# Two expert routings: the eight largest logits of a tile and their positions from VectorE, the router's bias by TensorE, the gather index ahead of the experts' table

## The chip, the cores and the metric

The kernel runs on one core of one Trainium2 chip. The metric is the device time of one execution in microseconds, as the median of several runs; lower is better. One execution was also taken by the profiler, and all the rows below come from it.

## The reference, cut to what matters

The input `x` holds T = 2048 tokens of width D = 256 (two sequences of 1024). Four blocks are added to it in turn:

```python
x = x + xattn0(layernorm(x), ctx)     # 16 heads of 64, 77 keys per sequence, RMS-normalised q and k
x = x + moe0(layernorm(x))            # 8 experts, hidden width 256, 2 experts per token
x = x + linear1(layernorm(x), ctx)    # x @ W1.T + mean(ctx) @ W2.T + b
x = x + moe1(layernorm(x))            # 8 experts, hidden width 1024, 2 experts per token
```

Each mixture of experts routes in the same way; only the second has a router bias:

```python
logits = x @ router_w (+ router_b)
probs = softmax(logits)
top_p, top_e = top_k(probs, 2)
y = sum over the token's two experts of top_p * (gelu(x @ w1[e] + b1[e]) @ w2[e] + b2[e])
```

## The kernel before, in words

Tokens stand in NT = 16 tiles of 128, one token per partition. A product of two numbers is made from fp16 halves, high and low, as three TensorE products (`three`), and weights are scaled by WS = 64. Each engine has one hand-written order of work, in software-pipelined loops over steps `s`; a function called with `s - 5` handles the tile that entered five steps earlier. Semaphores tie the engines together.

The stages in order of time are these. First the attention's keys and values are prepared. Then a loop over the 16 tiles (`for s in range(NT + 9)`, on every engine) does the query projection (`q_proj`), scores (`scores`, `shift`), exponentials, their sums (`sums`, L1124 to L1131, on VectorE), the normalisation of the weights by GpSimd (`norm_weights`, L648), transposes of the weights on TensorE with their split into halves by ScalarE (`pt_hi`, L857) and VectorE (`pt_lo`, L1136), the product with the values (`attn`), its addition to the residual (`add_attn`, L1146), the second layer norm's statistics (`stats`), and for an older tile the router's logits: TensorE's `logits(0, ln1, i)` at step i + 8 writes eight numbers per token into a small place of bank 5, and VectorE's `logits(0, i)` (L1153), in the same step, scales them into `lg`. `sums` ends with a reciprocal (L1130) and a multiplication by PS = 1024 (L1131). VectorE's `split_lo` (L1095) makes the low halves of expert weights in the odd steps, GpSimd's (L616) in the even ones.

Then comes `route(0)`. VectorE finds the largest logit, its place, the second largest and its place over all 16 tiles at once (L1235 to L1248, twelve linked operations), which ends in `hot`, a table of ones; then the two gates (L1255 to L1259). TensorE counts the tokens of each expert (RANKS). VectorE turns counts into places (L1267 to L1293), TensorE turns places into token numbers (`tokens_done`), VectorE makes the table of experts per slot (L1299 to L1304) and last the gather index (L1307). TensorE goes on with idle products (`idle_work`) meanwhile. GpSimd waits for the one semaphore `routed` and gathers rows by that index.

The first experts follow: 39 slots of 128 rows each. Four weight chunks are split first (L1095), then per slot VectorE copies the expert's weights (`first_weights`, L1370), TensorE transposes the gathered rows and multiplies, ScalarE does the gelu. SyncE's queue writes each slot's result (`keep_y`, L509) and loads the last big weight chunks (`stage`). Its loop over slots issues `stage(NCH - 1)` at the second-to-last slot step, ahead of the last five `keep_y`.

Then a loop over 16 tiles gathers the two results of each token (L712), adds them with their gates (L1444, L1450), applies the linear block (`add_linear`, L1432), layer norm, and the second router: TensorE's `logits(1, ln3, i)` at step i + 7, read by VectorE's `logits(1, i)` (L1157) at step i + 9, which adds the bias `rbb`. Then `route(1)` by the same code, and the second experts, 39 slots again, with `slot_weights` (L1333) on VectorE and scatter-adds into the output by GpSimd (L725).

VectorE's part of the attention loop, as far as order matters here:

```python
if LEAD <= s - 4 < NT:      # L1197
    pt_lo(s - 4, 0)
    pt_lo(s - 4, 1)
...
if 0 <= s - 6 < NT and (PRE + s - 6) % 2:      # L1207
    split_lo(PRE + s - 6)
```

Of the kernel before, what the change touches and what calls it, by code (L numbers as in the profile page):

```python
# [7 lines left out]
ALU = mybir.AluOpType  # L8
# [3 lines left out]
P = 128  # L12
# [51 lines left out]
def build(nc, x, ctx_t, wq, wk, wv, scale_q, scale_k, wo, bo, rw0, w_in0, b_in0, w_out0, b_out0,  # L64
# [29 lines left out]
    with ExitStack() as ctx:  # L94
# [104 lines left out]

        back = lg[:, :, :].rearrange("p t e -> p (t e)")[:, 0:NQS[1]].bitcast(U32)  # L200
# [132 lines left out]
        LOG = [bank[5][:, 400:400 + E]] * 2  # L333
        LOG1 = [bank[4][:, 400:400 + E], bank[5][:, 400:400 + E]]
# [83 lines left out]
        def _(sp):  # L418
# [96 lines left out]
            for j in range(NSLOTS[0] + 4):  # L515
# [35 lines left out]
        def _(pool):  # L551
# [41 lines left out]
            g.memset(pb2[:, NS:NS + 1], PS)  # L593
            g.memset(pb01[:, :, NS:NS + 1], PS)
# [9 lines left out]
            link(g.iota(first8[:, :], pattern=[[-1, E]], base=E, channel_multiplier=0,  # L604
# [82 lines left out]
            def slot_rows(layer):  # L687
                pool.wait_ge(sem("routed"), layer + 1)
# [52 lines left out]
        def _(act):  # L741
# [110 lines left out]
            def pt_hi(i, n):  # L852
                a, b = groups[n]
                act.wait_ge(sem("weights_tr"), NG * i + n + 1)
                if i >= 2:
                    act.wait_ge(sem("attn_done"), i - 1)
                s_.activation(pt[:, i % 2, 0, a:b, :], bank[6 + (NG * i + n) % 2][:, 0:(b - a) * P].rearrange(  # L857
                    "p (c t) -> p c t", t=P), ACT.Copy).then_inc(sem("pt_hi"), 1)
# [35 lines left out]
            def route(layer):  # L894
                act.wait_ge(sem("route_shift"), 2 * layer + 1)
                r = routes[layer]
                s_.activation(r[:, 7 * P:7 * P + NT * E], r[:, 0:NT * E], ACT.Exp).then_inc(sem("route_exp"), 1)
                act.wait_ge(sem("route_shift"), 2 * layer + 2)
                s_.activation(r[:, 1104:1104 + NT], r[:, 1152:1152 + NT], ACT.Exp).then_inc(sem("route_exp"), 1)
# [26 lines left out]
            act.wait_ge(sem("routed"), 1)  # L926
# [49 lines left out]
        def _(dve):  # L976
# [147 lines left out]
            def sums(i):  # L1124
# [5 lines left out]
                link(v.reciprocal(rs[:, i % 2, :], rs[:, i % 2, :]))  # L1130
                v.tensor_scalar(rs[:, i % 2, :], rs[:, i % 2, :], PS, None, ALU.mult).then_inc(sem("row_sums"), 1)  # L1131

            def pt_lo(i, n):
                a, b = groups[n]
                dve.wait_ge(sem("pt_hi"), NG * i + n + 1)
                v.tensor_tensor(pt[:, i % 2, 1, a:b, :], bank[6 + (NG * i + n) % 2][:, 0:(b - a) * P].rearrange(  # L1136
                    "p (c t) -> p c t", t=P), pt[:, i % 2, 0, a:b, :], ALU.subtract).then_inc(sem("pt_lo"), 1)
# [12 lines left out]
            def logits(layer, i):  # L1150
                dve.wait_ge(sem("logits_done"), NT * layer + i + 1)
                if layer == 0:
                    v.tensor_scalar(lg[:, i, :], LOG[i % 2], 1.0 / WS, None, ALU.mult).then_inc(sem("logits_read"), 1)  # L1153
                else:
                    if i == 0:
                        dve.wait_ge(sem("rb_loaded"), 16)
                    v.scalar_tensor_tensor(out=lg[:, i, :], in0=LOG1[i % 2], scalar=1.0 / WS, in1=rbb[:, :],  # L1157
                                           op0=ALU.mult, op1=ALU.add).then_inc(sem("logits_read"), 1)

            for s in range(NT + 9):  # L1160
# [21 lines left out]
                if 0 <= s - 8 < NT:  # L1182
                    logits(0, s - 8)
# [21 lines left out]
                if s == 3:  # L1205
                    split_lo(3)
                if 0 <= s - 6 < NT and (PRE + s - 6) % 2:  # L1207
                    split_lo(PRE + s - 6)

            def route(layer):  # L1210
# [10 lines left out]
                ex, m1, m2, best = cut(0), r[:, 1024:1024 + NT], r[:, 1152:1152 + NT], r[:, 1088:1088 + NT]  # L1221
                oh = [cut(1), cut(2)]
                cand, masked = cut(3), cut(4)
# [5 lines left out]
                cur = lg[:, :, :]  # L1229
                f8 = first8[:, None, :].to_broadcast([P, NT, E])  # L1230

                def all_experts(m):
# [638 lines left out]
```

## Time and profile before

| what | us |
|---|---|
| median of 3 runs | 650.48 |
| lowest, highest run | 647.2, 650.99 |
| the profiled execution, whole | 651.32 |
| its span, first to last instruction | 649.5 |
| mean granted TensorE clock in it, share of full speed | 0.931 |

The span is what the rows below divide up; around it lie 1.8 us of start and end. A row of a timeline gives start, duration, engine, line, operation, output <- input, shapes and count, and in brackets the idle time of that engine just before it and what released it. Unlinked instructions of one engine overlap in it by some hundredths of a microsecond.

### The profile page before, as it was taken

What the parts mean: (1) busy time and instruction counts of PE and PEld (TensorE: products, weight loads), DVE (VectorE), ACT (ScalarE), POOL (GpSimd) and SP (SyncE); (2) the same over time, 40 slices, a digit from 0 to 9 for tenths busy, and PEclk for the clock granted to TensorE, in tenths of its full rate; (3) what the DMA queues carried; (4) which work ended last, traced back from release to release, by engine and by line L of the source; (5) the groups of instructions that cost most, each with busy time, mean ns of one, the idle gap of its engine ahead of it and who ended that gap; (6) DMA issues with size and microseconds to landing.
All of it is one profiled execution on the core that took longest, in us unless ns stands there. A gap on an engine that the chain in (4) does not pass through costs nothing.

```text
span 649.5 us, 17761 instructions
## 1 busy us (share of the span) xinstructions
PE 537.8 (83%) x6478; PEld 482.4 (74%) x6478; DVE 522.7 (80%) x1052; ACT 369.4 (57%) x597; POOL 370.9 (57%) x300
## 2 busy tenths in 40 slices
PE   5899999999998754798981655299999999999991
PEld 4898898989898642677760444179999999999991
DVE  4877899999988859699986998777788777777861
ACT  3735476766755442799975788344444444444441
POOL 8157598898888622775505883044555565554332
PEclk9989999999988885899996799689999999999997
DMA  8600223333231344798772642544545544444422
GB/s 300 166 11 17 75 59 82 91 82 92 74 99 49 98 101 168 220 302 274 221 236 90 180 120 67 155 94 57 80 78 76 75 79 80 78 77 75 62 25 25
DMA packets 74228, 71.30 MB, mean 110 GB/s; under 512 B 44257, under 2 KB 64482, under 8 KB 73890
## 3 DMA queue, kind: packets, MB, share of 16 engines
q1 hardware_dynamic: 63250, 50.59, 27.7%
q0 software_dynamic: 10896, 19.58, 16.1%
q8 instruction: 56, 0.92, 0.6%
q14 instruction: 26, 0.21, 0.1%
HBM read 44.83 MB, written 16.53 MB: 94 GB/s over the span
## 4 chain that ended last, share of the span: by engine, by line
PE 45%; DVE 23%; issue 9%; ACT 8%; POOL 8%; DMA 4%; DVEq 1%; POOLq 0%; ACTq 0%; SPq 0%
PE banks L1491 43%; POOL heads L636 2%; DVE w_region L1141 2%; POOL w_region L643 2%; POOL w_region L648 2%; DMA out<-slot_region,lg 2%; DVE slot_region L1136 2%; DVE wb_region L1014 2%; DVE w_region L1128 1%; ACT wb_region L836 1%; PE banks L1710 1%; DVE heads L1111 1%; DVE w_region L1118 1%; ACT slot_region L906 1%; ACT wb_region L781 1%
## 5 line engine op out<-in xcount | busy, mean ns | idle before, releaser
L1491 PE MATMUL banks<-w_region,wb_region 128*128 (+1 forms) x1000 | 118.7, 276 | 10.0 <-DMA wb_region<-wk 7.5
L725 POOL DMA_INDIRECT out<-slot_region,lg x39 | 67.0, 1718 | 98.4 <-ACT slot_region L959 72.9
L1491 PE MATMUL banks<-w_region 128*128 128x128 f16 (+5 forms) x1484 | 111.3, 233 | 13.5 <-DVE w_region L1141 8.1
L1491 PEld LDWEIGHTS banks<-w_region 128*128 128x128 f16 (+3 forms) x1484 | 106.3, 127 | 18.7 <-DVE w_region L1141 11.7
L1491 PEld LDWEIGHTS banks<-w_region,wb_region 128*128 128x128 f16 (+1 forms) x1000 | 99.7, 105 | 20.5 <-issue 10.7
L1491 PE MATMUL banks<-slot_region,staging 128*128 128x128 f16 x1872 | 110.9, 219 | 0.9 <-ACT slot_region L906 0.7
L1491 PEld LDWEIGHTS banks<-slot_region,staging 128*128 128x128 f16 x1872 | 107.5, 98 | 2.2 <-ACT slot_region L906 0.9
L912 ACT ACTIVATE wb_region<-wb_region 128x1024 f32<-128x1024 f32 x39 | 41.3, 1058 | 90.2 <-DVE wb_region L1342 90.2
L1333 DVE COPY staging<-w_region 128x2048 f16 x78 | 57.3, 737 | 40.6 <-PE banks L1491 39.8
L681 POOL DMA_INDIRECT slot_region<-normed_rows,index x39 | 45.5, 1166 | 36.2 <-DVE index L1307 16.6
L1491 PE MATMUL banks<-w_region,slot_region 128*128 128x256 f16 x480 | 58.6, 283 | 1.9 <-DVE slot_region L1136 1.9
L681 POOL DMA_INDIRECT slot_region<-gated_rows,index x39 | 41.6, 1068 | 26.1 <-DVE index L1307 14.5
L1491 PEld LDWEIGHTS banks<-w_region,slot_region 128*128 128x128 f16 x480 | 48.2, 102 | 9.0 <-DVE slot_region L1136 2.0
L712 POOL DMA_INDIRECT wb_region<-sorted_y,slots x32 | 32.9, 1030 | 31.7 <-DMA sorted_y<-slot_region 23.6
L1491 PE MATMUL banks<-wb_region,w_region 128*128 (+1 forms) x302 | 49.0, 301 | 1.3 <-DVE w_region L1080 0.8
L636 POOL TENSOR_TENSOR heads<-heads,neghalf 128x16 f32<-128x16 f32 x16 | 47.7, 2983 | 2.5 <-DVE heads L1104 2.5
L1342 DVE SCALAR_TENSOR_TENSOR wb_region<-banks,b_s 128x1024 f32<-128x1024 f32 x39 | 47.2, 1209 | 1.1 <-PE banks L1491 1.1
L1349 DVE TENSOR_TENSOR wb_region<-wb_region 128x1024 f16<-128x1024 f32 x39 | 47.2, 1211 | 0.6 <-ACT wb_region L921 0.6
L648 POOL TENSOR_TENSOR w_region<-w_region 128x1232 f32<-128x1232 f32 x16 | 36.2, 2261 | 16.0 <-DVE w_region L1131 15.4
L857 ACT ACTIVATE slot_region<-banks 128x512 f16<-128x512 f32 (+1 forms) x48 | 23.5, 522 | 35.0 <-PE banks L1614 35.0
L921 ACT ACTIVATE wb_region<-wb_region 128x1024 f16<-128x1024 f32 x39 | 40.6, 1042 | 0.1
L643 POOL TENSOR_TENSOR w_region<-w_region,heads 128x1232 f32<-128x1232 f32 x16 | 38.5, 2406 | 1.3
(236 smaller groups left out, 1033.9 us busy)
## 6 DMA issues: line engine op xcount, KB each, us to landing
staging<-w_t SPq DMA_DIRECT2D x22, 512.0 KB, 4.3
sorted_y<-slot_region SPq DMA_DIRECT2D x39, 128.0 KB, 4.0
w_region<-w_t SPq DMA_DIRECT2D x8, 512.0 KB, 5.7
x_res<-x SPq DMA_DIRECT2D x4, 512.0 KB, 7.8
staging<-w_in SPq DMA_DIRECT2D x4, 512.0 KB, 3.7
normed_rows<-w_region SPq DMA_DIRECT2D x16, 128.0 KB, 1.9
staging<-w_out SPq DMA_DIRECT2D x4, 512.0 KB, 4.0
gated_rows<-wb_region SPq DMA_DIRECT2D x16, 128.0 KB, 2.2
```

The source lines that it names most:

```text
L636: link(g.tensor_tensor(v, v, neghalf[:, 0:1].to_broadcast([P, NH]), ALU.pow))
L643: g.tensor_tensor(p_rows(i), p_rows(i), rq[:, i % 2, :, None].to_broadcast([P, NH, L]), ALU.mult).then_inc(sem("scores_scaled"), 1)
L648: g.tensor_tensor(p_rows(i), p_rows(i), rs[:, i % 2, :, None].to_broadcast([P, NH, L]), ALU.mult).then_inc(sem("weights_ready"), 1)
L681: g.indirect_dma_start(out=m.rows[:, j % m.RING, a, :].bitcast((F16, U32)[layer]), out_offset=None, in_=rows_dram[layer], in_offset=bass.I ...
L712: g.indirect_dma_start(out=ring[:, i % n, c, :], out_offset=None, in_=y_dram, in_offset=bass.IndirectOffsetOnAxis(ap=slots[:, i, c:c + 1], ...
L725: g.indirect_dma_start(out=out, out_offset=bass.IndirectOffsetOnAxis(ap=back[:, j:j + 1], axis=0), in_=m.y[:, j % m.YB, 0, :], in_offset=N ...
L912: s_.activation(v, v, ACT.Gelu_apprx_tanh).then_inc(sem("gelu"), 1)
L921: s_.activation(m.hh[:, j % 2], v, ACT.Copy).then_inc(sem("h_hi"), 1)
L1333: v.tensor_copy(w_slot[:, :, half], src[:, :, half]).then_inc(sem("slot_weights"), 1)
L1342: v.scalar_tensor_tensor(out=m.g[:, j % 2], in0=hidden(m, j), scalar=1.0 / WS, in1=bias[:, :, None].to_broadcast([P, m.HC, m.SW]), op0=ALU ...
L1349: v.tensor_tensor(m.hl[:, j % 2], m.g[:, j % 2], m.hh[:, j % 2], ALU.subtract).then_inc(sem("h_lo"), 1)
L1491: return t.matmul(o, a, b, start=start, stop=stop)
```

## The change

The two routings no longer search all tiles at once. For each tile VectorE runs `max` (the eight largest values, sorted; of eight logits all of them) and `max_index` (their positions), straight from the PSUM banks where TensorE left the logits. The logits of the first ten tiles stay in one bank side by side, those of the last six in other banks, and VectorE's calls (`tops`) stand at the ends of the steps given by `tops_at`, from step 18 on. The reads of `lg` step by step are gone. The two tables of ones come from comparing positions with 0 to 7. The second router's bias enters as two products with an identity matrix, of its halves. In the first routing the gates are computed behind the index and the experts' table, in the second ahead of the counts. The gather index stands ahead of the experts' table, and `routed` counts twice per routing: GpSimd waits for the index, TensorE and ScalarE for both. The factor PS moves out of `sums` into `pt_hi` (as a scale) and `pt_lo` (a fused multiply and subtract), and the constant column of the weights is 1 instead of PS. `stage(NCH - 1)` moves behind the loop over slots.

```diff
+        SHARED = 10
+        def log_home(layer, i):
+            if i < SHARED:
+                return bank[(5, 2)[layer]][:, 384 + E * i:384 + E * (i + 1)]
+            return bank[((1, 2, 3, 4, 1, 2), (3, 3, 4, 5, 2, 3))[layer][i - SHARED]][:, 400 + E * (i % 2):400 + E * (i % 2 + 1)]
+        def bank_full(layer, i):
+            return SHARED if i < SHARED else max(i + 1, SHARED + 2 * layer)
+        def tops_at(layer, s):
+            if layer == 0:
+                return {NT + 2: range(0, 5), NT + 3: range(5, 10), NT + 4: range(10, 12), NT + 5: range(14, 15)}.get(s, ())
+            return {NT + 2: range(0, 3), NT + 3: range(3, 6), NT + 4: range(6, 10), NT + 5: range(10, 12),
+                    NT + 6: range(12, 14), NT + 7: range(14, 15), NT + 8: range(15, 16)}.get(s, ())
...
                 elif j == NSLOTS[0] - 1:
-                    stage(NCH - 1)
                     stage(NCH - LATE + 1)
                 if j >= 4:
                     keep_y(j - 4)
+            stage(NCH - 1)
...
-                link(v.reciprocal(rs[:, i % 2, :], rs[:, i % 2, :]))
-                v.tensor_scalar(rs[:, i % 2, :], rs[:, i % 2, :], PS, None, ALU.mult).then_inc(sem("row_sums"), 1)
+                v.reciprocal(rs[:, i % 2, :], rs[:, i % 2, :]).then_inc(sem("row_sums"), 1)
...
+            def tops(layer, tiles):
+                for i in tiles:
+                    dve.wait_ge(sem("logits_done"), NT * layer + bank_full(layer, i))
+                    sorted_at = mark(v.max(out=lg[:, i, :], in_=log_home(layer, i)))
+                if tiles:
+                    dve.wait_ge(sem("dve_chain"), sorted_at)
+                for i in tiles:
+                    v.max_index(out=ranked_of(layer)[:, i, :], in_max=lg[:, i, :], in_values=log_home(layer, i)).then_inc(
+                        sem("logits_read"), 1)
...
-                if 0 <= s - 8 < NT:
-                    logits(0, s - 8)
+                if s == NT + 5:
+                    tops(0, range(12, 14))
+                if s == NT + 7:
+                    tops(0, range(15, 16))
...
+                tops(0, tops_at(0, s))
                 if 0 <= s - 6 < NT and (PRE + s - 6) % 2:
                     split_lo(PRE + s - 6)
...
-                link(v.tensor_reduce(m1, cur, axis=AX.X, op=ALU.max))
...
-                v.tensor_tensor(hot.rearrange("p t e -> p (t e)"), oh[0], oh[1], ALU.add).then_inc(sem("hot"), 1)
+                for c in range(2):
+                    chosen = v.tensor_tensor(te(both[:, c, :]), ranks[:, c, :, None].to_broadcast([P, NT, E]),
+                                             first8[:, None, :].to_broadcast([P, NT, E]), ALU.is_equal)
+                    if c:
+                        link(chosen)
+                v.tensor_tensor(hot.rearrange("p t e -> p (t e)"), both[:, 0, :], both[:, 1, :], ALU.add).then_inc(
+                    sem("hot"), 1)
+                v.tensor_tensor(te(ex), lg[:, :, :], lg[:, :, 0:1].to_broadcast([P, NT, E]), ALU.subtract).then_inc(
+                    sem("route_shift"), 1)
...
+                if layer == 1:
+                    gates_of()
                 dve.wait_ge(sem("counts_done"), layer + 1)
...
+                dve.wait_ge(sem("tokens_done"), layer + 1)
+                found, later = bank[6][:, 0:NQ], bank[6][:, NQ:2 * NQ]
+                v.tensor_scalar(index[:, 0:NQ], found, -1.0, 0.0, ALU.add, ALU.max).then_inc(sem("routed"), 1)
                 if layer == 0:
                     link(v.tensor_scalar(slots[:, :, :], where, ALMOST_HALF, None, ALU.add))
...
-                link(v.tensor_scalar(expert[:, 1, 0:NSLOT], es, float(2 * DC * moes[layer].H), None, ALU.mult))
-                dve.wait_ge(sem("tokens_done"), layer + 1)
+                v.tensor_scalar(expert[:, 1, 0:NSLOT], es, float(2 * DC * moes[layer].H), None, ALU.mult).then_inc(
+                    sem("routed"), 1)
+                dve.wait_ge(sem("routed"), 2 * (layer + 1))
+                if layer == 0:
+                    gates_of()
...
-                if 0 <= s - 9 < NT:
-                    logits(1, s - 9)
+                tops(1, tops_at(1, s))
...
-                if i >= 7:
-                    pe.wait_ge(sem("logits_read"), i - 6)
...
+                for n in range(2 * layer):
+                    mm(home, ident_h[:, :], rb_halves[:, n, :], n == 0, False)
```

## Rows read from the trace of the kernel before

**Rows 1.** Stages: busy us of each engine, granted clock, DMA share, GB/s.
```profile
78.00:188.00 110.00, 105.44 (x1340) 99.66 (x1337) 103.64 (x194) 75.70 (x116) 96.80 (x57) 1.00 0.29 79
...
260.00:341.00 81.00, 69.46 (x860) 56.20 (x858) 72.51 (x173) 68.23 (x135) 41.94 (x38) 0.98 0.82 251
...
411.00:428.00 17.00, 7.28 (x63) 4.40 (x63) 13.16 (x39) 1.82 (x4) 3.07 (x4) 0.54 0.47 135
428.00:618.00 190.00, 189.48 (x2601) 179.63 (x2602) 150.33 (x216) 91.62 (x109) 96.84 (x70) 1.00 0.49 76
```

**Rows 2.** The chain of waits by engine, whole span.
```profile
PE 45%; DVE 23%; issue 9%; ACT 8%; POOL 8%; DMA 4%; DVEq 1%; POOLq 0%; ACTq 0%; SPq 0%
```

**Rows 3.** The chain of waits, two steps of the attention loop: start, us, what.
```profile
104.66 0.18 DVE w_region L1131
...
104.92 2.25 POOL w_region L648
...
116.71 0.07 DVE lg L1153
```

**Rows 4.** VectorE's timeline, a step of the attention loop.
```profile
206.75 0.15 DVE L1153 TENSOR_SCALAR lg<-banks 128x8 f32<-128x8 f32 x1
206.83 1.11 DVE L1111 TENSOR_REDUCE heads<-banks 128x12 f32<-128x924 f32 x1
```

**Rows 5.** VectorE's timeline, first routing.
```profile
242.76 0.17 DVE L1153 TENSOR_SCALAR lg<-banks 128x8 f32<-128x8 f32 x1 [0.44 <-PE banks L1491]
242.96 0.29 DVE L1235 TENSOR_REDUCE w_region<-lg 128x16 f32<-128x128 f32 x1
...
246.52 0.29 DVE L1248 TENSOR_TENSOR w_region<-w_region 128x128 f16<-128x128 f32 x1
246.74 0.28 DVE L1255 TENSOR_REDUCE w_region<-w_region 128x16 f32<-128x128 f32 x1
...
248.12 0.17 DVE L1267 TENSOR_SCALAR w_region<-banks 128x8 f32<-128x8 f32 x1 [0.61 <-PE banks L1491]
...
255.65 0.20 DVE L1307 TENSOR_SCALAR index<-banks 128x39 uint32<-128x39 f32 x1
```

**Rows 6.** VectorE's timeline, the end of the attention loop (steps 18 to 20).
```profile
221.66 1.27 DVE L1136 TENSOR_TENSOR slot_region<-banks,slot_region 128x512 f16<-128x512 f32 x2
224.22 0.43 DVE L1146 SCALAR_TENSOR_TENSOR x_res<-banks,x_res 128x256 f32<-128x256 f32 x1 [1.28 <-PE banks L1491]
...
229.31 1.22 DVE L1095 SCALAR_TENSOR_TENSOR w_region<-staging,w_region 128x1024 f16<-128x1024 f32 x1
```

**Rows 7.** TensorE's timeline at the last tile's attention product, and that stretch's clock.
```profile
232.12 5.11 PE L1491 MATMUL banks<-w_region,slot_region 128*128 128x256 f16 x30 [1.94 <-DVE slot_region L1136]
...
232.00:234.00 2.00, 1.88 (x9) 1.30 (x10) 0.29 (x3) 1.51 (x3) 1.90 (x3) 0.54 0.58 221
```

**Rows 8.** TensorE's timeline, the last token products, and the third slot's transposes.
```profile
254.19 0.71 PE L1491 MATMUL banks<-w_region 128*128 128x39 f16 x16 [0.35 <-DVE w_region L1293]
...
265.38 0.40 PE L1710 MATMUL banks<-ident_h,slot_region 128*128 128x128 f16 x4 [2.41 <-DMA slot_region<-normed_rows,index]
```

**Rows 9.** The chain of waits at the first experts' end, and DMA issues with landing.
```profile
340.71 3.28 DMA sorted_y<-slot_region
...
normed_rows<-w_region SPq DMA_DIRECT2D x16, 128.0 KB, 1.9
```

**Rows 10.** VectorE's timeline, the second router's loop and routing.
```profile
395.89 0.69 DVE L1014 TENSOR_TENSOR wb_region<-wb_region 128x256 f16<-128x256 f32 x1 [0.18 <-ACT wb_region L781]
...
403.26 0.41 DVE L1432 SCALAR_TENSOR_TENSOR x_res<-banks,x_res 128x256 f32<-128x256 f32 x1
...
405.60 0.42 DVE L1432 SCALAR_TENSOR_TENSOR x_res<-banks,x_res 128x256 f32<-128x256 f32 x1
...
410.87 0.17 DVE L1157 SCALAR_TENSOR_TENSOR lg<-banks,rbb 128x8 f32<-128x8 f32 x1 [0.71 <-PE banks L1491]
...
414.63 0.29 DVE L1248 TENSOR_TENSOR slot_region<-slot_region 128x128 f16<-128x128 f32 x1
```

More of the change, by code:

```diff
@@ L857, in pt_hi @@
                 s_.activation(pt[:, i % 2, 0, a:b, :], bank[6 + (NG * i + n) % 2][:, 0:(b - a) * P].rearrange(
-                    "p (c t) -> p c t", t=P), ACT.Copy).then_inc(sem("pt_hi"), 1)
+                    "p (c t) -> p c t", t=P), ACT.Copy, scale=PS).then_inc(sem("pt_hi"), 1)
             for s in range(NT + 9):
@@ L1135, in pt_lo @@
                 dve.wait_ge(sem("pt_hi"), NG * i + n + 1)
-                v.tensor_tensor(pt[:, i % 2, 1, a:b, :], bank[6 + (NG * i + n) % 2][:, 0:(b - a) * P].rearrange(
-                    "p (c t) -> p c t", t=P), pt[:, i % 2, 0, a:b, :], ALU.subtract).then_inc(sem("pt_lo"), 1)
+                v.scalar_tensor_tensor(out=pt[:, i % 2, 1, a:b, :], in0=bank[6 + (NG * i + n) % 2][
+                    :, 0:(b - a) * P].rearrange("p (c t) -> p c t", t=P), scalar=PS, in1=pt[:, i % 2, 0, a:b, :],
+                    op0=ALU.mult, op1=ALU.subtract).then_inc(sem("pt_lo"), 1)
             def q_lo(i):
@@ L1148, in add_attn, with ranked_of @@
                 dve.wait_ge(sem("attn_added"), i + 1)
[L1150 to L1158, printed above, removed]
+            def ranked_of(layer):
+                return routes[layer][:, 3 * P:3 * P + NT * E].bitcast(U32).rearrange("p (t e) -> p t e", e=E)
+            def tops(layer, tiles):
[7 more added lines that the diff above has]
+                        sem("logits_read"), 1)
             for s in range(NT + 9):
@@ L1303, in route @@
                 link(v.tensor_copy(expert[:, 0, 0:NSLOT], es))
-                link(v.tensor_scalar(expert[:, 1, 0:NSLOT], es, float(2 * DC * moes[layer].H), None, ALU.mult))
-                dve.wait_ge(sem("tokens_done"), layer + 1)
-                found, later = bank[6][:, 0:NQ], bank[6][:, NQ:2 * NQ]
-                v.tensor_scalar(index[:, 0:NQ], found, -1.0, 0.0, ALU.add, ALU.max).then_inc(sem("routed"), 1)
+                v.tensor_scalar(expert[:, 1, 0:NSLOT], es, float(2 * DC * moes[layer].H), None, ALU.mult).then_inc(
+                    sem("routed"), 1)
+                dve.wait_ge(sem("routed"), 2 * (layer + 1))
+                if layer == 0:
+                    gates_of()
                 if layer == 1:
@@ L1438, in _ @@
                 split_lo(k)
+            dve.wait_ge(sem("rb_loaded"), 16)
+            link(v.tensor_scalar(rb_halves[:, 0, :], rbb[:, :], WS, None, ALU.mult))
+            link(v.scalar_tensor_tensor(out=rb_halves[:, 1, :], in0=rbb[:, :], scalar=WS, in1=rb_halves[:, 0, :],
+                                        op0=ALU.mult, op1=ALU.subtract))
             for s in range(NT + 9):
```

82 lines of the change are left out of this document (34 added, 48 removed).

## The prediction

> **What bounds the kernel now.** I read the stages first, then the chain of waits, then each engine's timeline where the change touches it. From 428 to 618 us TensorE is busy 189.5 of 190 us at a granted clock of 1.00, its 2.4 GHz level, so the second experts are a fixed block that only starts earlier or later [rows 1]. The chain agrees: TensorE 45%, VectorE 23% of the span [rows 2]. In the attention loop (78 to 188) no engine alone is the bound: TensorE is busy 105.4, VectorE 103.6, GpSimd 96.8 of 110 us [rows 1], and the chain passes from VectorE's sums to GpSimd's normalisation and back [rows 3]. In a routing (411 to 428) TensorE is busy 7.3 of 17 us and VectorE 13.2: a serial chain of small VectorE operations with TensorE waiting, so what is cut there moves everything behind it [rows 1]. The first experts (260 to 341) have VectorE 72.5, TensorE 69.5 of 81 us, DMA 0.82 [rows 1]; nothing in their steady part changes.
>
> The sum is made against the profiled execution's 651.32 us (span 649.5 and 1.8 around it), which lies 0.84 above the median 650.48.
>
> **Attention loop: two operations less on the chain.** The chain shows the multiplication by PS 0.18 long with its link directly ahead of GpSimd's normalisation [rows 3]; without it GpSimd starts about 0.20 earlier. This sits on the chain once in two steps, five times between 78 and 188. The read of the logits appears on it with 0.07, four times [rows 3]. Together 5 x 0.20 + 4 x 0.07 = 1.3 us gained. In the other step of each pair GpSimd is itself still busy when the sums come, so nothing more is gained there. The scale in `pt_hi` and the fused `pt_lo` keep their shapes; I cost them at nothing. Bounds: 0 (another wait takes over) to 2.6.
>
> **The price of one tile's search.** No row of before shows `max` or `max_index`. The second takes in eight values and then searches the bank, so I count a tile as three small steps. Unlinked 128x8 steps start 0.08 apart (206.75, then 206.83), though each lasts 0.15 [rows 4]; linked small steps stand 0.20 apart (242.76, then 242.96) [rows 5]. So a tile costs between 0.16 (two steps of 0.08) and 0.60. I take 0.27, three steps of 0.09, nearest to rows 4 because within `tops` nothing is linked but the one wait between the two loops, which I put at 0.1 per group.
>
> The Trainium skill, "VectorE: DVE Perf Modes", § The DRAIN you can't avoid and § Rules for kernel authors, says that the next VectorE operation starts only when the last one's pipe is empty, and to keep the count of operations small: with full lengths of 0.155 a tile would cost 0.47. Rows 4, with 0.08 between starts, speak against that for short steps; what it would make of the time is the second rival's nearer half.
>
> **First routing, the end of the attention loop.** Ten of the 16 searches stand where VectorE is waited for.
> - Step 18: five tiles, 5 x 0.27 + 0.1 = 1.45, between `pt_lo` (221.66 to 222.93) and `add_attn` at 224.22, ahead of which VectorE idles 1.28 [rows 6]. With one logits read (0.08) gone, 0.1 is left over.
> - Step 19: 1.45 ahead of `split_lo` at 229.31 [rows 6]. What follows, `add_attn` and `pt_lo` of the last tile, is what TensorE waits for with 1.94 idle before 232.12 [rows 7]; so 1.45 - 0.08 = 1.4 late.
> - TensorE's product at 232.12 takes 5.11 with a granted clock of 0.54 in its first 2 us, mostly the 1.2 GHz level [rows 7]. Idle longer before it, it may run more of it there: at 1.2 GHz throughout, 30 x 256 columns are 6.4 us, an estimate from the shape in that row. I take 0.3 of the possible 1.3.
> - Tiles 10 to 14 fall into waits of VectorE, but tile 14 stands ahead of `split_lo` (1.22) and must wait for logits that come after it now; so that the last tile's search starts 0.55 late. Itself it takes 0.25 more than the 0.20 of the read it replaces (three dependent steps).
> - The twelve linked operations from 242.96 to the end of `hot` at 246.81 are 3.85 us [rows 5]. Left are two comparisons and one addition, 0.22 + 0.33 + 0.29 = 0.84: 3.0 gained.
> - The gates (from 246.74 to the start of the 0.61 of idle, 0.8 us [rows 5]) were hidden behind TensorE's counts; behind the index they delay only VectorE's weight splits.
> - The index: token products end at 254.90 [rows 8], the index ran at 255.65 [rows 5]. In front of the table it is 0.65 earlier.
>
> Sum to the index: 0.1 + 1.4 + 0.3 + 0.55 + 0.25 - 3.0 - 0.65 = -1.05. The gathers follow; the third slot waits 2.41 on its gather [rows 8]. VectorE itself, with table and gates behind the index, comes free earlier only by some 1 us less than the gathers, and it has to copy weights for the first slot; I take 0.35 off: -0.7.
>
> **End of the first experts.** `stage(NCH - 1)`, 512 KB, shared the DMA engines with the last results: the last `keep_y` takes 3.28 on the chain [rows 9]. An equal transfer of 128 KB, the `normed_rows` writes, takes 1.9 [rows 9]. Behind the loop on SyncE's queue the load no longer runs ahead of five `keep_y`. 1.0 gained of at most 1.4; its cover is the wait for the first gathered results, and if ScalarE's split came later than that, 1 us would be lost instead.
>
> **Second routing.** In the loop before it VectorE waits 0.18 for ScalarE in each step [rows 10], so dropping the logits reads gains nothing. At its end, three tiles at 0.91 (with the wait) stand ahead of `add_linear` at 403.26 and three ahead of that at 405.60 [rows 10], each less 0.08: about 1.5 late, since the layer norm of the last tile follows from them. Bias products: 0.1 on the last tile. The last search: 0.25 more. From 411.07, 0.20 behind the last read, to the end of `hot` at 414.92 [rows 10] 3.85 become 0.84: -3.0. The gates now end 0.2 behind the counts, because the exponential starts later; the index gains 0.25, because the table already hid most of that wait. Sum: 1.5 + 0.1 + 0.25 - 3.0 + 0.2 - 0.25 = -1.2.
>
> **Sum.** -1.3 - 0.7 - 1.0 - 1.2 = -4.2: 647.1 against 651.32; against the median 650.48, 646.3.
>
> **The rivals.**
> 1. *The searches hide better and are cheaper.* At 0.18 a tile (two short steps), step 18 hides wholly, step 19 costs 0.9, the second loop's groups 1.0 instead of 1.5, and the last tiles 0.1 less each: 1.3 less in all. With the loop's gain at its bound, 2.6, it is 2.6 more than forecast: 643.7. For it: rows 4. Against: a search of eight numbers for eight values is hardly one short step.
> 2. *The searches are slow and become the end of both loops.* At 0.60 a tile a group of five is 3.1: step 18 costs 1.7, step 19 3.0, the clock 0.8, the last tile 1.2, against 3.65 gained: +3.0 where I have -0.7. In the second loop groups of three are 1.9, so 3.7 late, and the nine tiles behind them (5.4) outlast the last logits by 2: with the same other terms about +3.2 where I have -1.2. Total 646.3 + 3.7 + 4.4 = 654.4, slower than before. It decides from about 0.45 a tile on, where the total is zero. At the skill's 0.47 the time would be the same as before. For it: linked steps at 0.20 [rows 5], and the order of work that puts ten tiles ahead of awaited operations [rows 6]. Against: nothing links them.
> 3. *The shorter first routing does not reach the slots.* The slots follow VectorE's splits, or the gathers land no earlier because the loads move with them; and the last `keep_y` keeps its 3.28. Then the two gains 3.65 and 1.0 are spent on less: +0.7 + 1.0, 648.0; with a loop gain of 0 also, 649.3. For it: VectorE's 72.5 of 81 us in that stage [rows 1]. Against: the wait of 2.41 on a gather [rows 8].
>
> **How the numbers follow.** Forecast 0.50, rival 1 0.25, rival 2 0.10, rival 3 0.15. The range reaches from 641.5 (rival 1 and the keep of 1.4, and clock dips of 1 to 2 us that fall differently) to 651.0, which leaves out most of rival 2 and some of the deepest gains. A measurement of this kernel, whose three runs lie within 0.6%, tells about 1% from no change. Faster by over 1% means under 644.0: half of rival 1 and some of the forecast, 0.24. Slower by over 1% means over 657.0: only the far part of rival 2, 0.05. The rest is 0.71.
>
> **What would show it.** Right: between a tile's searches starts about 0.09 apart; `hot` 0.84 behind the last search; the index directly behind `tokens_done`; the attention product of the last tile about 1.5 later against its loop, in a loop 0.27 shorter per two steps; the last `keep_y` near 2.3. Wrong: starts 0.2 apart, a `split_lo` of the last steps several us late, the first slots waiting on VectorE's copies instead of gathers, or an attention loop with an unchanged period.

## The result, and the profile after

The changed kernel takes 640.48 us (median of four runs, 640.08 to 642.68) against 650.59 for the kernel before in the same comparison: the recorded ratio is 0.9868, 95% interval 0.9834 to 0.9903 (the two medians alone, of four runs each, divide to 0.984). The forecast was 646.3 with a range from 641.5. So the direction was right and the gain, 10.1 instead of 4.2, more than twice as large; the median lies 1 us under the lower end of the range. The profiled execution took 640.1, its span is 638.4, the mean granted clock 0.933.

The stages of the changed kernel (columns as in [rows 1]; the attention loop 1 us earlier than there, the first experts 7 and in 80 us instead of 81, the second routing and the second experts 11), and its chain by engine:

```profile
77.00:187.00 110.00, 105.73 (x1343) 99.90 (x1340) 102.40 (x177) 76.29 (x117) 97.84 (x57) 1.00 0.29 80
253.00:333.00 80.00, 68.58 (x862) 54.95 (x859) 75.14 (x175) 68.65 (x135) 41.31 (x37) 1.00 0.81 251
400.00:417.00 17.00, 8.93 (x84) 5.48 (x84) 12.62 (x45) 2.94 (x5) 4.29 (x6) 0.53 0.52 149
417.00:607.00 190.00, 189.57 (x2602) 179.73 (x2603) 150.55 (x215) 91.55 (x108) 95.01 (x70) 1.00 0.47 76
```

```profile
PE 45%; DVE 21%; POOL 10%; issue 9%; ACT 9%; DMA 4%; DVEq 1%; POOLq 0%; ACTq 0%; SPq 0%
```

The second experts are the same block of 189.6 busy us, only earlier, and VectorE's share of the chain falls from 23% [rows 2] to 21%. VectorE's timeline shows the searches and the short routing, to be laid beside [rows 5, 6]:

```profile
218.25 0.45 DVE L1178 MAX8 lg<-banks 128x8 f32<-128x8 f32 x5
218.73 0.09 DVE L1182 MATCH_VALUE_LOAD w_region<-lg,banks 128x8 f32 x1
218.81 0.17 DVE L1182 FIND_INDEX8 w_region<-lg,banks 128x8 uint32<-128x8 f32 x1
218.89 0.07 DVE L1182 MATCH_VALUE_LOAD w_region<-lg,banks 128x8 f32 x1
...
219.79 0.42 DVE L1167 SCALAR_TENSOR_TENSOR x_res<-banks,x_res 128x256 f32<-128x256 f32 x1 [0.26 <-PE banks L1518]
...
224.89 0.46 DVE L1178 MAX8 lg<-banks 128x8 f32<-128x8 f32 x5
...
226.10 1.21 DVE L1116 SCALAR_TENSOR_TENSOR w_region<-staging,w_region 128x1024 f16<-128x1024 f32 x1
...
238.59 1.21 DVE L1116 SCALAR_TENSOR_TENSOR w_region<-staging,w_region 128x1024 f16<-128x1024 f32 x1
239.71 0.17 DVE L1178 MAX8 lg<-banks 128x8 f32<-128x8 f32 x1
...
240.72 0.29 DVE L1263 TENSOR_TENSOR w_region<-w_region 128x128 f16<-128x128 f32 x1
...
249.14 0.20 DVE L1318 TENSOR_SCALAR index<-banks 128x39 uint32<-128x39 f32 x1 [0.81 <-PE banks L1518]
```

A group of five runs from 224.89 to 226.10, 1.21 in all: five maxima in 0.46, then a pair for each position, 0.14 from start to start. The first group leaves VectorE 0.26 of its 1.28 idle ahead of tile 13's addition; the second stands wholly ahead of the split at 226.10. Tile 14's split (238.59) does delay the last maximum, as feared. `hot` ends 1.3 behind the start of the last maximum, and the index comes directly behind the token products.

The chain in the attention loop has one small operation less ahead of GpSimd, as against [rows 3]:

```profile
103.64 0.27 DVE w_region L1151
103.90 0.07 issue
103.97 2.25 POOL w_region L670
```

TensorE's timeline at the first slots, against [rows 8]: the first slot waits for VectorE's copy of its weights, and the third slot's transposes have no wait at all.

```profile
254.14 0.40 PE L1740 MATMUL banks<-ident_h,slot_region 128*128 128x128 f16 x4 [0.22 <-DMA slot_region<-normed_rows,index]
256.78 0.84 PE L1518 MATMUL banks<-slot_region,w_region 128*128 128x128 f16 x12 [2.25 <-DVE w_region L1394]
257.59 0.38 PE L1740 MATMUL banks<-ident_h,slot_region 128*128 128x128 f16 x4
```

VectorE's timeline at the second loop's end, against [rows 10]: two groups of three ahead of awaited additions, and the gates waiting 0.37 for the exponential.

```profile
393.28 0.31 DVE L1178 MAX8 lg<-banks 128x8 f32<-128x8 f32 x3
...
394.07 0.41 DVE L1456 SCALAR_TENSOR_TENSOR x_res<-banks,x_res 128x256 f32<-128x256 f32 x1
...
403.20 0.29 DVE L1263 TENSOR_TENSOR slot_region<-slot_region 128x128 f16<-128x128 f32 x1
...
404.07 0.29 DVE L1275 TENSOR_REDUCE slot_region<-slot_region 128x16 f32<-128x128 f32 x1 [0.37 <-ACT slot_region L919]
```

**A shift that no edit made.** Two traces can be compared landmark by landmark. Between the two first ones TensorE's clock differs where nothing was changed. The stretch of the attention loop in the kernel before, in its first profile (columns as in [rows 1]):

```profile
190.00:192.00 2.00, 2.00 (x24) 2.00 (x24) 2.00 (x4) 1.11 (x1) 0.82 (x2) 0.80 0.62 176
192.00:194.00 2.00, 2.00 (x21) 1.94 (x22) 1.22 (x4) 0.60 (x2) 0.81 (x1) 0.50 0.24 94
194.00:196.00 2.00, 2.00 (x22) 2.00 (x20) 1.97 (x6) 1.97 (x3) 1.54 (x2) 0.50 0.00 0
```

and the same stretch in its second profile (`e0`, below):

```profile
192.00:194.00 2.00, 2.00 (x37) 1.99 (x37) 1.93 (x7) 1.16 (x2) 0.43 (x1) 1.00 0.41 156
194.00:196.00 2.00, 2.00 (x35) 1.96 (x33) 1.97 (x3) 1.94 (x4) 2.00 (x2) 1.00 0.00 0
```

TensorE is busy throughout these rows in both, yet in the first it gets 0.50, its 1.2 GHz level, from 192 to 198 us, and does 21 products in 2 us instead of 37. TensorE's idle time just before, 0.93 of the 2 us from 188, is the same in the second profile (0.94). The reductions over the heads just behind it on VectorE come 1.9 later, counted as in the table below. No edit stands between the two profiles. So the second profile is the one to compare with.

Each kernel's timeline also starts differently (tile 0's addition lies between 77.7 and 81.9 us in the eleven traces). The table therefore counts from that addition: for each landmark (the start of an instruction on VectorE's timeline) it gives the time in the changed kernel, and how much later it comes in the other runs.

| landmark | changed | before (e0) | e1 | e2 | e3 | e8 | e4 | e5 | e7 |
|---|---|---|---|---|---|---|---|---|---|
| addition of tile 13 | 142.08 | +1.33 | 0.00 | 0.00 | +0.29 | +0.11 | +0.99 | +0.03 | -0.36 |
| addition of tile 14 | 149.52 | +0.11 | -0.02 | -0.01 | -0.92 | -1.11 | +2.29 | -1.18 | -2.18 |
| addition of tile 15 | 156.00 | +0.46 | +0.13 | -0.05 | -0.57 | -0.78 | +1.66 | -2.49 | -2.91 |
| first `hot` | 163.01 | +2.71 | +0.12 | -0.05 | +1.78 | +1.48 | +2.61 | -2.91 | -3.14 |
| first index | 171.43 | +3.43 | +0.12 | +0.53 | +1.77 | +1.49 | +2.61 | -2.90 | -3.13 |
| first `add_linear` | 270.56 | +5.37 | +1.37 | +1.12 | +2.88 | +1.16 | +3.10 | -2.60 | -2.60 |
| 13th `add_linear` | 309.54 | +5.82 | +1.45 | +1.29 | +3.35 | +1.62 | +3.10 | -2.58 | -2.62 |
| last `add_linear` | 318.97 | +4.76 | +1.45 | +1.29 | +2.29 | +0.55 | +4.92 | -3.57 | -3.61 |
| second `hot` | 325.49 | +7.46 | +1.44 | +1.29 | +4.79 | +3.26 | +7.20 | -3.56 | -3.59 |
| second index | 334.17 | +7.69 | +1.44 | +1.39 | +4.79 | +3.25 | +7.20 | -3.57 | -3.59 |
| VectorE's last | 549.99 | +8.61 | +0.86 | +0.64 | +4.62 | +3.05 | +7.83 | -2.65 | -4.40 |

e6 has no column; its rows are named where they are used. Up to the first edit that touches them, the rows agree to 0.05, but for 0.13 in e1, whose product of tile 15 lasts 4.92 instead of 4.78, and up to 0.2 between e3 and e8, which have the same code as far as the first `hot`. From the second index to the end no kernel differs in code, yet the distances change by up to 0.9 either way: that much no edit explains, and it is called chance here. The gain that the traces show is 8.6; the medians say 8.3 to 10.1, because the kernel before itself gave 650.59 in the first comparison and 648.8 to 649.0 (13 to 19 runs each) in the three later ones.

### The profile page after: what moved, and what is told of

Its sections match the earlier page's. It is cut to its first block, busy times and chain, and to the rows that moved or that the text cites. A ratio compares the mean times of both kernels' runs of the same rounds, so it can differ in the third digit from the quotient of the medians.

```text
span 638.4 us, 17846 instructions
## 1 busy us (share of the span) xinstructions
PE 537.2 (84%) x6510; PEld 480.6 (75%) x6510; DVE 521.5 (82%) x1086; ACT 368.6 (58%) x595; POOL 368.1 (58%) x300
## 4 chain that ended last, share of the span: by engine, by line
PE 45%; DVE 21%; POOL 10%; issue 9%; ACT 9%; DMA 4%; DVEq 1%; POOLq 0%; ACTq 0%; SPq 0%
PE banks L1518 43%; POOL heads L658 3%; POOL w_region L665 2%; POOL w_region L670 2%; DMA out<-slot_region,lg 2%; DVE w_region L1162 2%; DVE slot_region L1156 2%; DVE wb_region L1035 1%; ACT wb_region L858 1%; DVE w_region L1149 1%; ACT wb_region L803 1%; DVE heads L1132 1%; ACT slot_region L927 1%; DVE w_region L1139 1%; POOL slot_region L703 1%
## 5 line engine op out<-in xcount | busy, mean ns | idle before, releaser
L1518 PE MATMUL banks<-w_region 128*128 128x128 f16 (+5 forms) x1484 | 108.4, 229 | 12.3 <-DVE w_region L1162 6.9
L1518 PEld LDWEIGHTS banks<-w_region 128*128 128x128 f16 (+3 forms) x1484 | 103.4, 125 | 17.5 <-DVE w_region L1162 10.4
L703 POOL DMA_INDIRECT slot_region<-normed_rows,index x39 | 44.1, 1130 | 32.7 <-DVE index L1318 13.7
```

What stands on the lines that cost most here:

```text
L703: g.indirect_dma_start(out=m.rows[:, j % m.RING, a, :].bitcast((F16, U32)[layer]), out_offset=None, in_=rows_dram[layer], in_offset=bass.I ...
L1518: return t.matmul(o, a, b, start=start, stop=stop)
```

## The experiments

Ratios are to the kernel before, in the same comparison.

**e0, the kernel before again.** No edit.

> The kernel before, unchanged, profiled a second time. In the first profile TensorE's granted clock fell to about 0.5 between 191 and 198 us of the attention loop although TensorE was never idle there, and that stretch is 2.1 us longer than in the changed kernel. Theory A (the dip comes and goes from run to run): the second profile has no dip there, and the heads' reductions near 203 to 207 us start about 2 us earlier than 206.9. Theory B (the dip belongs to the order of work of the kernel before): it returns at the same place within 3 us and the span is again near 649.5.

648.78, ratio 1.000 (0.997 to 1.003). The dip is gone (rows above), as theory A has it. So it was not the change that removed it.

**e1, the load back in the loop.**

```diff
                 elif j == NSLOTS[0] - 1:
+                    stage(NCH - 1)
                     stage(NCH - LATE + 1)
...
-            stage(NCH - 1)
```

> The changed kernel with stage(NCH - 1) back inside the loop over slots, as before. Theory A (the load competed with the last keep_y): the last keep_y takes about 3 us instead of 1.69 again and everything behind it comes 1.0 to 1.6 later, near 641.8. Rival B (the transfer was hidden, and ScalarE's split of that chunk, which now comes 1.2 late, gives the gain back): no difference, 640.5.

641.66, ratio 0.9888 (0.9859 to 0.9917): by time not to be told from the changed kernel. The chain at the first experts' end, first in the changed kernel, then in e1, then in e0:

```profile
332.14 1.69 DMA sorted_y<-slot_region
```

```profile
332.30 3.94 DMA sorted_y<-slot_region
```

```profile
338.37 2.11 DMA sorted_y<-slot_region
```

In e1 the last `keep_y` takes 2.25 longer, and the first `add_linear` comes 1.25 later against the index: theory A. But the price is not a fixed one. With the load ahead of it this `keep_y` takes 2.11 (e0), 2.94 (e6), 3.28 [rows 9] and 3.94 (e1); with the load behind the loop it takes 1.69 or 1.70 in all seven traces.

**e2, the index behind the table.**

```diff
-                dve.wait_ge(sem("tokens_done"), layer + 1)
-                found, later = bank[6][:, 0:NQ], bank[6][:, NQ:2 * NQ]
-                v.tensor_scalar(index[:, 0:NQ], found, -1.0, 0.0, ALU.add, ALU.max).then_inc(sem("routed"), 1)
                 if layer == 0:
                     link(v.tensor_scalar(slots[:, :, :], where, ALMOST_HALF, None, ALU.add))
...
                     sem("routed"), 1)
+                dve.wait_ge(sem("tokens_done"), layer + 1)
+                found, later = bank[6][:, 0:NQ], bank[6][:, NQ:2 * NQ]
+                v.tensor_scalar(index[:, 0:NQ], found, -1.0, 0.0, ALU.add, ALU.max).then_inc(sem("routed"), 1)
                 dve.wait_ge(sem("routed"), 2 * (layer + 1))
                 if layer == 0:
                     gates_of()
...
-                pool.wait_ge(sem("routed"), 2 * layer + 1)
+                pool.wait_ge(sem("routed"), 2 * layer + 2)
```

> The changed kernel with the first routing's index behind the table of experts and the gates, so that the index is 1.6 to 1.7 later than at 249.14 while VectorE comes free at the same time or 0.8 earlier. The second routing is treated the same way without the gates, there the index is about 1.5 later. Theory A (the first slots follow the gathers): slots of the first experts start 1.0 to 1.7 later, and the second experts, which also wait for gathers, 0.5 to 1.5; together 642 to 643.5. Theory B (VectorE's copies of weights set the first slots, as the forecast assumed when it took 0.35 off): the first experts start at the same time, at most 0.5 lost in all, 640.5 to 641.

641.44, ratio 0.9865 (0.9835 to 0.9895): not separable from the changed kernel by time. The index is only 0.53 later, not 1.6, since the table fills VectorE's wait for the token products and the gates, against the expectation's wording, stay behind it. But the first `add_linear` is 1.12 later: the slots lose twice what the index loses, so the index's own delay is not the whole of it. VectorE's splits start 0.94 behind the index there instead of 2.62, and the third gather takes 1.95 instead of 1.19; what that means, e3 and e8 show.

**e3, everything but the searches and the bias products.** The kernel before with PS moved, the load behind the loop and the index ahead of the table; gates still ahead of the counts.

> The kernel before with every part of the change but the searches and the bias products: PS moved, the load behind the loop, index ahead of the table; the reads of the logits and the twelve linked operations stay. By the working the searches are worth, net, about 0.3 in the attention loop, 1.4 in the first routing (2.7 at the linked chain less 1.2 at step 19 less 0.5 at tile 14, and 0.4 of smaller terms) and 1.5 in the second. Theory A: 3.2 slower than the changed kernel, near 643.7. Rival B (the searches give back in front of the last tiles what they gain behind them): within 1 of the changed kernel, 640.5 to 641.5.

646.98, ratio 0.997 (0.9935 to 1.0005). By the traces it stands 4.8 behind the changed kernel at the second index, more than theory A's 3.2. Up to the first index 1.77 of it arises, as worked out. Then 1.11 more appears in the first slots, where there is no search at all. VectorE's and GpSimd's timelines there, with TensorE's third slot:

```profile
255.22 2.36 DVE L1095 SCALAR_TENSOR_TENSOR w_region<-staging,w_region 128x1024 f16<-128x1024 f32 x2
255.51 1.77 POOL L681 DMA_INDIRECT slot_region<-normed_rows,index  x1 [0.30 <-issue]
...
257.50 2.35 DVE L1095 SCALAR_TENSOR_TENSOR w_region<-w_region 128x1024 f16<-128x1024 f32 x2
257.59 1.95 POOL L681 DMA_INDIRECT slot_region<-normed_rows,index  x1 [0.30 <-issue]
...
262.38 0.57 PE L1712 MATMUL banks<-ident_h,slot_region 128*128 128x128 f16 x4 [1.29 <-DMA slot_region<-normed_rows,index]
```

GpSimd's second and third gather take 1.77 and 1.95 where a later one takes 0.95. Both start just after one of VectorE's weight splits. VectorE's four splits themselves start 1.14 apart, with the gathers beside them.

**e8, the gates moved too.** e3 with one edit:

```diff
+                def gates_of():
...
+                if layer == 1:
+                    gates_of()
                 dve.wait_ge(sem("counts_done"), layer + 1)
...
                 dve.wait_ge(sem("routed"), 2 * (layer + 1))
+                if layer == 0:
+                    gates_of()
```

> The kernel of e3_no_search (everything but the searches and the bias products) with one part more of the change: the first routing's gates move from their place ahead of the counts to behind the index and the table of experts. VectorE's four weight splits then start 0.8 later against the index (2.6 instead of 1.9 behind it). In e3 GpSimd's second and third gather took 1.77 and 1.95 beside the splits and the third slot waited 1.29; in the changed kernel, with the splits 0.8 later, they took 0.96 and 1.19 and nothing waited. Theory A (the gates hold the splits back until the first gathers are out): the second and third gather take about 1.0 and 1.2 again, the third slot no longer waits, and from the index to the first gathered result of the second loop it is 1.1 less than in e3, near 645.9. Rival B (GpSimd's pace has another cause, and the forecast was right that later splits only cost): the gathers stay at 1.8 and 1.9 and the slots come at the same time or up to 0.8 later, 647 to 647.8.

645.25, ratio 0.9943 (0.992 to 0.9967), 1.7 under e3; the two intervals overlap, so the reading rests on the traces. The same view of it, with TensorE's third and fourth slot:

```profile
253.96 0.96 POOL L681 DMA_INDIRECT slot_region<-normed_rows,index  x1 [0.30 <-issue]
...
254.37 2.35 DVE L1095 SCALAR_TENSOR_TENSOR w_region<-staging,w_region 128x1024 f16<-128x1024 f32 x2
255.23 1.18 POOL L681 DMA_INDIRECT slot_region<-normed_rows,index  x1 [0.30 <-issue]
...
256.71 1.97 POOL L681 DMA_INDIRECT slot_region<-normed_rows,index  x1 [0.30 <-issue]
...
260.20 0.38 PE L1717 MATMUL banks<-ident_h,slot_region 128*128 128x128 f16 x4
...
261.46 0.40 PE L1717 MATMUL banks<-ident_h,slot_region 128*128 128x128 f16 x4 [0.20 <-DMA slot_region<-normed_rows,index]
```

The second gather now starts ahead of the first split and takes 0.96, the third 1.18, and only the fourth 1.97; the third slot's transposes no longer wait, the fourth slot's wait 0.20. What the forecast feared is there too: the first slot's products start 7.62 behind the index instead of 6.93, because VectorE's copies come later. But the third slot's start 0.6 earlier and the fourth's 1.3, and from the index to the first `add_linear` it takes 1.44 less than in e3, where 1.1 was expected. Theory A. What is left between e8 and the changed kernel is the searches and the bias alone: 3.25 at the second index. The medians, from two comparisons, put 4.8 between them; the traces place the rest in the start (1.14) and behind VectorE's last instruction, where the two do not differ in code.

**e6, the weight loads behind the third slot.** The kernel before with

```diff
-                        sp.wait_ge(sem("slot_tr"), j + 1)
+                        sp.wait_ge(sem("slot_tr"), max(j + 1, 3))
```

> The kernel before with one edit that is no part of the change: the weight loads that start at the first slot wait for the third slot's transposes instead of the first one's. In the kernel before the third slot waits 2.06 and 2.41 (two profiles) for its gather, which is issued beside those loads (512 KB each); in the changed kernel that gather is issued 1.3 ahead of them and nothing waits. Theory A (the loads took the DMA engines from the third gather, and the earlier index only won that race): the wait falls under 0.7 and the slots from the third on start 1.3 to 2 earlier, near 647.3. Rival B (the gathers are late by GpSimd's own pace, 1.7 to 2 each): the wait stays above 1.5 and the time does not change, 648.8.

649.27, ratio 0.9995 (0.9974 to 1.0016). GpSimd's second gather and TensorE's third slot in it:

```profile
256.28 1.67 POOL L681 DMA_INDIRECT slot_region<-normed_rows,index  x1 [0.30 <-issue]
...
262.15 0.40 PE L1710 MATMUL banks<-ident_h,slot_region 128*128 128x128 f16 x4 [1.29 <-DMA slot_region<-normed_rows,index]
```

The third slot's wait falls from 2.06 (e0) to 1.29, the two first gathers stay at 1.95 and 1.67, and the median does not change; from the index to the first `add_linear` the trace has 0.5 less than e0's. Neither theory whole: the loads made 0.8 of that wait. The rest is left beside the slow gathers; that these cause it is argued here, and e8 bears on it.

**e4, every group searched twice.**

```diff
+                for again in range(2):
...
+                    if again == 0:
+                        for i in tiles:
+                            found_at = mark(v.max_index(out=ranked_of(layer)[:, i, :], in_max=lg[:, i, :],
+                                                        in_values=log_home(layer, i)))
+                        if tiles:
+                            dve.wait_ge(sem("dve_chain"), found_at)
```

> The changed kernel with every group of searches run twice (the second result replaces the first, so nothing but time is added). A group of five took 1.2 in the changed kernel's trace (five maxima 0.45, five pairs 0.14 apart), 0.21 a tile and 0.1 a group. Theory A (ten of the 16 searches of each routing stand where VectorE is waited for): 1.05 more before the addition of tile 13 (1.3 less the 0.26 that VectorE idles there), 1.3 at step 19, 0.6 at tiles 14 and 15; in the second loop 1.65 for the two groups of three and about 1.0 for the rest; 5 to 6 in all, near 646. Rival B (VectorE's waits swallow them): under 2, below 642.5.

648.88, ratio 1.0004 (0.9988 to 1.0021); 7.2 behind the changed kernel at the second index: theory A and more. The terms come out about as written at step 18 (+0.99), step 19 (+1.30) and in the groups of three (+1.82); the second loop's tail costs 2.28 instead of 1.0. Only tile 15's product gave 0.6 back: the low clock fell on tile 14's.

**e5, the searches in VectorE's waits.**

```diff
+                if s == NT + 3:
+                    tops(0, range(0, 5))
+                if s == NT + 4:
+                    tops(0, range(5, 10))
+                if s == NT + 5:
+                    split_lo(PRE + s - 6)
                 if 0 <= s - 6 < NT:
                     norm_lo(ln1, s - 6)
...
+                tops(1, {NT + 2: range(0, 4)}.get(s, ()))
                 if 0 <= s - 3 < NT:
                     norm_lo(ln2, s - 3)
+                tops(1, {NT + 3: range(4, 5), NT + 4: range(5, 6)}.get(s, ()))
```

The same searches leave `tops_at`, and the last split leaves its old place.

> The changed kernel with the same searches put into VectorE's waits: the groups of five of the first routing ahead of the waits of 1.78 for ScalarE's layer norm in the next two steps, the split of the last step ahead of that step's layer norm, and in the second loop four tiles into the wait of 1.12 for ScalarE and one into each wait of 0.36 for the roots. Theory A (the forecast's step 19 and second loop are real costs): 1.2 less at step 19, 0.45 at the last tile, 0.75 twice in the second loop, 3.1 in all, near 637.4. Rival B (the waits only move, since the same engines meet again at the next tile): within 1 of the changed kernel.

637.97, ratio 0.983 (0.9798 to 0.9861), an interval that overlaps that of the changed kernel; by the traces 3.6 ahead of it at the second index. Theory A, though not by its terms alone. Step 19 is earlier by 1.18, the last tile by 0.42, the second loop by 1.0 where 1.5 was expected. VectorE's wait for ScalarE ahead of `norm_lo` shrinks from 1.78 to 0.57 and still covers the group:

```profile
222.28 0.46 DVE L1178 MAX8 lg<-banks 128x8 f32<-128x8 f32 x5
...
224.15 0.42 DVE L1035 TENSOR_TENSOR w_region<-w_region 128x256 f16<-128x256 f32 x1 [0.57 <-ACT w_region L803]
```

Another 1.3 is the clock's: tile 15's product ran at full clock and took 3.45 instead of 4.78,

```profile
228.65 3.45 PE L1526 MATMUL banks<-w_region,slot_region 128*128 128x256 f16 x30 [1.95 <-DVE slot_region L1156]
```

though TensorE idled 1.95 ahead of it, as long as in the kernel before, where the clock fell [rows 7]. In e7 the idle time was shorter, 1.37. Why the clock held in e5 stays open.

**e7, two more edits.** e5 with the split of step 19 one step later, the first routing's groups of five one step earlier than in e5, and e6's edit.

> The changed kernel with the searches in VectorE's waits and two more edits: the split that stood ahead of tile 14's addition moves one step on, into the next wait of 1.78 (its place is then free and the second group of five takes the wait before), and the first weight loads wait for the third slot's transposes. Theory A: the 3.1 of the searches in the waits and 1.1 for that split, 4.2 in all, near 636.3; the loads' wait changes nothing here, since the gathers are already ahead of them. Rival B (what is gained ahead of tile 15 is met by ScalarE or by the clock after a longer idle): 1 to 3 gained, 637.5 to 639.5.

637.59, ratio 0.9824 (0.9797 to 0.9851). Tile 14's addition comes 1.0 earlier than in e5 but tile 15's only 0.4 and the index 0.2: between the two VectorE waits 1.25 for ScalarE's layer norm instead of 0.57, as rival B has it.

```profile
229.95 1.25 DVE L1035 TENSOR_TENSOR w_region<-w_region 128x256 f16<-128x256 f32 x1 [1.25 <-ACT w_region L803]
```

e5 and e7 cannot be told apart by time. Both are faster than the kernel before. That they are faster than the changed kernel too is shown by their traces (3.6 at the second index) and by medians of another comparison, 2.5 and 2.9 lower.

## Why the prediction was right in direction and wrong in size

Point by point against e0, forecast first:

- **Attention loop, -1.3: measured -1.33.** e3 keeps the reads and moves PS; at the addition of tile 13 it stands 0.29 behind the changed kernel for the reads, which leaves 1.04 for PS. The forecast had 0.28 and 1.0: both terms were right.
- **Step 18, +0.1, and step 19, +1.4: measured 0.0 and +1.22.** A tile cost 0.21 where I took 0.27; at the 0.47 that the Trainium skill's rule (VectorE: DVE Perf Modes, § The DRAIN you can't avoid) would make of it, a group would have been 2.5, and the trace has 1.2. That section of the Trainium skill adds that a next operation that is not held starts earlier, and the 0.07 between these starts go with that. [rows 4] was the right neighbour, and e4 shows that the price per tile is a real one, so rival 2 failed on its size alone.
- **The clock, +0.3: measured -0.35.** This step failed in sign. TensorE's last attention product in the changed kernel, and the clock around it:

```profile
228.90 4.78 PE L1518 MATMUL banks<-w_region,slot_region 128*128 128x256 f16 x30 [3.15 <-DVE slot_region L1156]
```

```profile
228.00:229.00 1.00, 0.10 (x1) 0.11 (x2) 0.77 (x4) 0.07 (x1) 0.41 (x1) 0.62 0.54 147
229.00:230.00 1.00, 1.00 (x6) 0.69 (x6) 0.00 (x0) 0.46 (x1) 0.90 (x3) 0.50 0.87 320
...
231.00:232.00 1.00, 1.00 (x8) 0.78 (x7) 1.00 (x3) 0.00 (x0) 0.59 (x1) 0.67 0.00 0
```

  TensorE idled 3.15 ahead of it instead of 1.94 [rows 7]. The clock fell to 0.50 while TensorE was still idle, at about 228.2, so part of the slow stretch ran over nothing. I had reckoned with a longer slow stretch in the product, up to 6.4 us for the whole of it at 1.2 GHz; no run has that, the longest product took 5.12, and here the stretch only began earlier. In e5 and e7 it did not come in this product at all (3.45), in e4 one tile sooner, so the product lasts between 3.45 and 5.12 from kernel to kernel, and the term was not to be had from the trace of before.
- **Last tile, +0.8, and `hot`, -3.0: measured -2.25 together** (forecast -2.2), and the index -0.72 (forecast -0.65). Right.
- **First slots, 0.35 off: measured between -0.7 and -1.5.** The largest failed step. From the index to the first `add_linear` the changed kernel gains 1.94, and the load has a share of that: 1.25 by e1, only 0.42 by the last `keep_y` of e0 itself. In e3, which moves the index and the load but not the gates, 0.83 of it is there; so the index by itself lies between a loss of 0.4, near the forecast, and a gain of 0.4. But I costed the gates' move as a delay of VectorE's splits and so as a loss. e8 shows that this delay is worth 1.44, and that the gathers beside the splits are shorter with it. The searches, the step from e8 to the changed kernel, give 0.33 back.
- **The load, -1.0: measured between -0.4 and -1.25.** The wait was the right one; its size differs from trace to trace.
- **Second loop's reads, nothing: measured -0.45.** The first eight or so reads were not covered by the wait of 0.18 [rows 10]: the starts of `norm_lo` are 3.28 apart in the kernel before from the step in which the reads begin, 3.21 in the changed one. That wait was what remained beside them, not a cover for them.
- **Second loop's end, +1.5, and the rest to the index, -2.7: measured +1.06 and -2.93.** The groups again at 0.21 a tile instead of 0.27; the gates' 0.37 of waiting ended with the counts, as worked out.
- **Not forecast:** 0.92 in the second experts, which differ by as much where the code is the same.

The sum of the terms is -8.6 where I had -4.2. Of the difference 1.3 come from the slots and the load together, 1.05 from the first routing (the clock 0.65 of it), 0.9 from the second loop, 0.9 are chance and 0.3 small ones. Rival 1 had cheap searches right and no other of these. Rival 3 is refuted by the table: the earlier routing reached the slots more than in full.

## What to carry to other kernels

An operation put ahead of a semaphore that many wait for is not free because it runs beside a transfer: price it by the wait that is really left, and move it into a wait that the timeline shows, as e5 did for 2.2 of its 3.6 us (the clock gave the rest). When two engines both become free at a point, ask not only who is late but whom the earlier one then disturbs. Compare two traces from a common landmark on, and profile the kernel before twice: 2 of the 11 us between the first two spans belonged to a clock dip in one profile.

## What was not expected of the hardware

**GpSimd's gathers take longer beside VectorE's splits.** A gather with nothing beside it takes 0.95 to issue. One that starts while a split of 1.2 is under way takes what is left of that split and 0.8 more. In e3 a pair of splits begins at 255.22 and lasts 2.36, so the first ends near 256.4; the gather from 255.51 ends at 257.28. The next pair begins at 257.50, its first ends near 258.7; the gather from 257.59 ends at 259.54. In e8 the third gather starts at 255.23, some 0.35 ahead of its split's end, and takes 1.18. In the changed kernel eleven gathers start with 0.31 to 1.15 of a split left, and each takes 0.81 or 0.82 more than that; one of them:

```profile
295.53 1.22 DVE L1116 SCALAR_TENSOR_TENSOR w_region<-staging,w_region 128x1024 f16<-128x1024 f32 x1
296.11 1.46 POOL L703 DMA_INDIRECT slot_region<-normed_rows,index  x1 [1.04 <-PE banks L1740]
```

The Trainium skill, SBUF — State Buffer, § SBUF: two separate sides, says that the two engines share a pair of ports as an exclusive lock, which a VectorE operation with two SBUF inputs, as a split is, and a GpSimd operation that reads SBUF hold for a whole instruction; it goes to whichever starts first, and the other waits. On GpSimd's side these rows agree, and so does the gather that begins just ahead of a split and is not slowed (0.96 in e8). On VectorE's side they do not: the split that begins at 254.37 in e8, inside that gather, takes 1.22 like any other, and the next one starts 1.14 behind it. That the lock is the cause is argued from these times; e8 shows only that moving the splits changes the gathers.

**A search is cheap.** Five maxima of eight numbers on 128 partitions take 0.45, 0.07 apart; loading eight values and finding their positions takes 0.14 from start to start, 0.21 a tile in all.

**The clock can fall under a busy TensorE.** It was at 0.50 from 192 to 198 us of one profile, with TensorE busy all that time, and in no other of the eleven traces at that place. The idle time just ahead was the same in e0, where it did not fall. What set it off stays open.
